# Key-key products of a head moved into its own step of a pipelined delta-rule decoder kernel

## What is computed

```
q = l2norm(causal_conv_silu(x @ Wq)); k, v alike, two of each per token   # 8 heads of 128
beta = 2 * sigmoid(x @ Wb); g = -exp(A_log) * softplus(x @ Wa + dt_bias)
for each token t:
    state = state * exp(g_t)
    for j in range(2):
        u = (v_j - k_j @ state) * beta_j
        state = state + outer(k_j, u)
    o_t = q_t @ state
out = (rmsnorm(o) * norm_w * silu(x @ Wg)) @ Wo
```

## Time and profile before

| | us |
|---|---|
| median of 3 runs | 946.26 |
| the profiled execution | 951.51 |
| its span on the core | 949.5 |
| TensorE busy (matrix products) | 849.2 |
| VectorE busy | 527.4 |
| ScalarE busy | 391.3 |
| POOL busy | 348.5 |

### The profile page before, as it was taken

One profiled execution on the slowest core, in us unless ns is written; L12 is line 12 of the kernel. 1 busy time (PEld: TensorE's weight loads), 2 busy tenths in 40 slices (PEclk: granted clock), 3 DMA queues, 4 the chain that ended last, 5 costly groups with the idle time before them and its releaser, 6 DMA issues.

```text
span 949.5 us, 16704 instructions
## 1 busy us (share of the span) xinstructions
PE 849.2 (89%) x5816; PEld 597.6 (63%) x5817; DVE 527.4 (56%) x1221; ACT 391.3 (41%) x839; POOL 348.5 (37%) x654
## 2 busy tenths in 40 slices
PE   4869999999999999999999876874999999999992
PEld 3344566766766856866667765763666677667762
DVE  3664747878868868878778764465511111111113
ACT  2736746655654654565565323102222222222220
POOL 0158268357555564573682570003330000000005
PEclk9987999999999999999999995797999999999997
DMA  8221230131031021021201301009563001100104
GB/s 206 73 41 27 72 81 8 17 78 17 9 79 23 11 70 23 13 67 24 51 2 23 90 1 28 1 1 374 213 223 134 28 28 33 33 29 26 33 23 127
DMA packets 102595, 57.91 MB, mean 61 GB/s; under 512 B 64192, under 2 KB 98048, under 8 KB 102528
## 3 DMA queue, kind: packets, MB, share of 16 engines
q1 hardware_dynamic: 99488, 51.62, 19.8%
q0 software_dynamic: 1536, 4.20, 1.4%
q10 hardware_dynamic: 1504, 1.20, 0.4%
HBM read 42.45 MB, written 14.55 MB: 60 GB/s over the span
## 4 chain that ended last, share of the span: by engine, by line
PE 76%; DVE 10%; ACT 6%; issue 4%; POOL 2%; DMA 1%; SPq 0%; POOLq 0%; ACTq 0%; DVEq 0%
PE bank L1598 16%; PE bank L581 13%; PE bank L1643 9%; PE bank L715 3%; PE bank L589 3%; DVE y L1053 3%; PE bank L749 3%; PE bank L640 3%; PE bank L700 3%; PE bank L719 2%; PE bank L714 2%; PE bank L595 2%; PE bank L1630 2%; PE bank L674 2%; PE bank L686 2%
## 5 line engine op out<-in xcount | busy, mean ns | idle before, releaser
L1053 DVE SCALAR_TENSOR_TENSOR y<-bank,cwh,y 128x510 f32<-128x510 f32 (+2 forms) x240 | 177.6, 744 | 78.9 <-ACT y L836 75.2
L581 PE MATMUL bank<-xnT,wbuf 128*128 128x512 f32 x320 | 165.2, 642 | 5.3 <-DVE y L1053 4.7
L1598 PE MATMUL bank<-f_wgu,f_xgT 128*128 x368 | 118.8, 466 | 0.0
L1857 DVE TENSOR_TENSOR f_act<-f_sg,bank 128x352 f32<-128x352 f32 x62 | 32.2, 521 | 143.8 <-PE bank L1598 141.4
L1369 POOL TENSOR_TENSOR term<-inv,blk 128x126 f32<-128x126 f32 (+22 forms) x248 | 87.8, 354 | 43.9 <-DMA blk<-a_blocks 25.1
L1932 POOL DMA_INDIRECT f_back<-slots_y,f_slot x16 | 15.4, 963 | 231.4 <-DMA slots_y<-f_yb 224.8
L581 PEld LDWEIGHTS bank<-xnT,wbuf 128*128 128x128 f32 x320 | 57.4, 199 | 66.8 <-issue 53.7
L1372 POOL TENSOR_TENSOR inv<-inv,term 128x126 f32<-128x126 f32 (+22 forms) x248 | 91.6, 369 | 19.4
L1705 ACT ACTIVATE f_sg<-bank 128x352 f32<-128x352 f32 x62 | 28.7, 464 | 161.0 <-PE bank L1598 152.7
L1643 PE MATMUL bank<-f_wdn,f_actT 128*128 (+1 forms) x372 | 91.5, 388 | 0.9 <-ACT f_actT L1718 0.8
L1598 PEld LDWEIGHTS bank<-f_wgu,f_xgT 128*128 128x128 f32 x368 | 66.2, 190 | 36.8 <-issue 7.6
(11 more groups left out here) (208 smaller groups left out, 1585.2 us busy)
## 6 DMA issues: line engine op xcount, KB each, us to landing
f_wgu<-in_exp_gu SPq DMA_DIRECT2D x8, 1408.0 KB, 8.6
f_wdn<-in_exp_dn SPq DMA_DIRECT2D x8, 640.0 KB, 9.7
blk<-a_blocks SPq DMA_DIRECT2D x16, 256.0 KB, 3.9
slots_x<-oT SPq DMA_DIRECT2D x24, 128.0 KB, 1.8
f_xg<-slots_x SPq DMA_DIRECT2D x24, 128.0 KB, 2.0
slots_y<-f_yb SPq DMA_DIRECT2D x23, 128.0 KB, 1.7
a_blocks<-aT SPq DMA_DIRECT2D x64, 32.0 KB, 1.6
inverses<-inv SPq DMA_DIRECT2D x16, 128.0 KB, 3.0
```

Of the source, the lines that this page charges most:

```text
L581: last = mm(bankA[p % 2][:, :], wbuf[A.par][:, kt, wblk, :], xnT[:, kt, (p % 2) * 512:(p % 2 + 1) * 512], start=kt == 0, stop=kt == 1)
L1053: v.scalar_tensor_tensor(out=y[p % 2][:, :, k:], in0=src[:, :, 0:SEQ - k], scalar=cwh[A.par][:, cb, 3 - k:4 - k], in1=y[p % 2][:, :, k:], ...
L1598: last = mm(gu[c][:, 0:FFH], xt[:, k, :], wgu[:, e, k, at:at + FFH], start=k == 0, stop=k == 1)
L1857: v.tensor_tensor(av[:, par, half * FFH:(half + 1) * FFH], sg[:, half, :], gu[2 * half + 1][:, 0:FFH], ALU.mult).then_inc(f_act, 1)
```

## The change

Gram leaves FIRST and is done for head A in slots 9 and 10 of its own step, once its four key projections are through. For this the key norms come two slots sooner (products in pairs behind projections 5 and 7, squares in pairs, sums and beta on VectorE in slot 8), and turn_blocks moves from slot 9 to slot 8, behind them. aT gets two buffers, since head A's products are masked while head B's are still read. p32, t32 and x32 each move a slot ahead, out items 2 and 3 move, kend and gate go one slot ahead. SP's gather is done for A at the step's end, behind scatter(B). POOL's `out_rms` moves into the inversion, ahead of round 12. The lines left out give aT its two buffers, aT0 and aT1, and let the products read `aT[par]`.

```diff
@@ -102,23 +102,24 @@
 FIRST, LAST = "first", "last"
-FILL = {FIRST: {"B": four("gram") + four("qk")},
+FILL = {FIRST: {"B": four("qk")},
         0: {"A": [("dx", 0), ("dx", 1), ("ex", 0), ("ex", 1)]},
...
         5: {"B": [("vtok", 3)]},
-        6: {"B": [("kend", 0)]},
-        7: {"E": [("out", 2)]},
-        8: {"B": [("kend", 1)]},
-        9: {"B": [("gate", 0)]},
-        10: {"B": [("p32", 0), ("p32", 1)], "E": [("out", 3)]},
-        11: {"B": [("t32", 0), ("t32", 1), ("kend", 2)]},
-        LAST: {"B": [("x32", 0), ("x32", 1), ("gate", 1), ("p64", 0), ("p64", 1), ("t64", 0), ("t64", 1)]}}
+        6: {"B": [("kend", 0)], "E": [("out", 2)]},
+        7: {"B": [("kend", 1)]},
+        8: {"B": [("gate", 0)]},
+        9: {"B": [("p32", 0), ("p32", 1)], "A": [("gram", 0), ("gram", 1)]},
+        10: {"B": [("t32", 0), ("t32", 1)], "A": [("gram", 2), ("gram", 3)]},
+        11: {"E": [("out", 3)], "B": [("x32", 0), ("x32", 1), ("kend", 2)]},
+        LAST: {"B": [("p64", 0), ("p64", 1), ("gate", 1), ("t64", 0), ("t64", 1)]}}
 PLACES = [FIRST] + list(range(12)) + [LAST]
...
 B_BANKS = 3
+RMS_AT = 12
@@ -254,6 +255,8 @@
     m8 = sb("m8", [P, 8])
+    aT1 = sb("aT1", [P, BATCH, CH, MU])
+    aT = [aT0, aT1]
     thr = t["thr"]
@@ -436,14 +439,14 @@
-        def gather(B):
+        def gather(A):
             for u in range(2):
-                sp.wait_ge(at_done, 4 * B.h + 2 * u + 2)
+                sp.wait_ge(at_done, 4 * A.h + 2 * u + 2)
                 for q in range(BLOCKS):
                     rows_ = slice(q * NB, (q + 1) * NB)
-                    sp.dma_start(diag[q][:, 8 * u:8 * u + 8, :], aT[rows_, 2 * u:2 * u + 2, :, rows_].rearrange("p b c n -> p (b c) n")).then_inc(a_out, 16)
-            sp.wait_ge(a_out, 32 * BLOCKS * (B.h + 1))
+                    sp.dma_start(diag[q][:, 8 * u:8 * u + 8, :], aT[A.par][rows_, 2 * u:2 * u + 2, :, rows_].rearrange("p b c n -> p (b c) n")).then_inc(a_out, 16)
+            sp.wait_ge(a_out, 32 * BLOCKS * (A.h + 1))
             for k in range(2):
@@ -459,8 +462,6 @@
         def step(A, B, C, E):
-            if B:
-                gather(B)
             if A and A.h < HEADS - 1:
@@ -484,6 +485,8 @@
                 scatter(B)
+            if A:
+                gather(A)
             if s == 1:
@@ -772,12 +775,13 @@
                     mix_turn(slot - 2)
-                if A and 6 <= slot < 10:
-                    norm(A, slot - 6)
                 if s == 0 and slot == 0:
...
                     proj(A, slot)
+                if A and slot in (5, 7):
+                    norm(A, slot - 5)
+                    norm(A, slot - 4)
                 if A and slot == 11:
@@ -875,7 +879,7 @@
                 act.wait_ge(oss_mm, A.h - 1)
-            act.wait_ge(silu_done, 10 * A.h + (4 if i < 4 else 6))
+            act.wait_ge(silu_done, 10 * A.h + (3 if i < 2 else 4 if i < 4 else 6))
             src = kraw[:, i * 512:(i + 1) * 512] if i < 4 else qraw[:, (i - 4) * 512:(i - 3) * 512]
@@ -987,8 +991,9 @@
                     silu(A, slot - 2)
-                if A and 5 <= slot <= 10:
-                    square(A, slot - 5)
+                if A and slot in (4, 6, 8):
+                    square(A, slot - 4)
+                    square(A, slot - 3)
                 if A and slot < 10:
@@ -1114,7 +1119,7 @@
                     dve.wait_ge(dm_done, 2 * B.h + 2)
-                v.tensor_tensor(aT[:, b, :, :].rearrange("p c (t j) -> p (c t) j", j=2), bank.rearrange("p (t j) -> p t j", j=2),
+                v.tensor_tensor(aT[B.par][:, b, :, :].rearrange("p c (t j) -> p (c t) j", j=2), bank.rearrange("p (t j) -> p t j", j=2),
                                 dx[:, b * CH:(b + 1) * CH, :].rearrange("p c (n a) -> p (c n) a", a=1).to_broadcast([P, CH * STEPS, 2]),
@@ -1250,11 +1255,11 @@
                     mix_add(slot - 3)
-                if B and slot == 9:
-                    turn_blocks(B)
-                if A and slot == 10:
+                if A and slot == 8:
                     norm_sum(A, 0)
                     fold_beta(A)
+                if B and slot == 8:
+                    turn_blocks(B)
                 if A and slot == 11:
@@ -1358,11 +1363,13 @@
-        def invert(B):
+        def invert(B, E):
...
             for j in range(NB - 1):
+                if j == RMS_AT and E:
+                    out_rms(E)
                 r, k = j // 2 + 1, NB - 1 - j
@@ -1377,10 +1384,10 @@
                 start(A)
-            if E:
+            if B:
+                invert(B, E)
+            elif E:
                 out_rms(E)
-            if B:
-                invert(B)
             if A:
...
                     pool.wait_ge(scal_done, 4)
```

More of the change, by code:

```diff
@@ L233, in attention @@
     gm = sb("gm", [P, BC // 2, STEPS])
-    aT = sb("aT", [P, BATCH, CH, MU])
+    aT0 = sb("aT0", [P, BATCH, CH, MU])
     TT = [sb(f"TT{i}", [P, BATCH, CH, MU]) for i in range(2)]
@@ L660, in item @@
                 m = n * (BC // 2) + k
-                a_m, t_m = aT[:, m // CH, m % CH, :], TT[par][:, m // CH, m % CH, :]
+                a_m, t_m = aT[par][:, m // CH, m % CH, :], TT[par][:, m // CH, m % CH, :]
                 cols = slice(k * STEPS, (k + 1) * STEPS)
```

## The result

The changed kernel takes 960.16 us (median; 955.31 to 964.43), the kernel before, run beside it on the same chip, 945.99 (943.99 to 947.09). The ratio is 1.0139, with a 95% interval of 1.0091 to 1.0186. The sign of the forecast holds (slower), the size does not: +6.0 us was forecast, +14.2 measured, and 960.2 lies 1.2 us above the range of 942 to 959.

The account below looks back on a forecast made before the run. TensorE was taken to bound the kernel, busy 849.2 of 949.5 us. Terms -4.6 + 1.0 + 9.0 + 0 - 4.5 + 4.5 = +5.4, +6.0 with kend's bank, put on the median 946.3 gave 952.2 us; range 942 to 959.

Parts of the forecast that it names:

- Part 1: Start of step 1: POOL's chain starts sooner, so TensorE's wait for gm shrinks; 4.6 us gained, bounds 2.5 to 5.
- Part 2: Slots 8 and 9: TensorE's p32 waits 1.5 us for X1 in steps 2 to 7, 9.0 us, plus 1.0 in step 1.
- (c): VectorE's slot 8: X1 is in time because TensorE runs later there; 937.7 us, faster; chance 0.10.
- (d): X1's two transposes are slowed by POOL's dx multiplication, 0 to 1.9 us in seven steps; 959 us; chance 0.10.
- Rival (e): Late masks on VectorE keep the inversion from coming forward, step 8 gives nothing; 956.7 us; within the forecast's 0.50.
- Part 3: Step boundary: a wait of 0.7 us replaces the 0.68, the dx wait stays; 0 per step, bounds -0.2 and +0.5.
- Part 4: Reordered queues, such as step 1's similarity tiles behind the gather and the scalars on POOL: no cost, with little cover.
- Part 5: Step 8: the 7.37 us X1 wait goes, a wait for U comes, half clock stays; 4.5 us gained.
- rival (b): Step 8: TensorE's clock is back to full, 9 us less; 943.2 us; chance 0.15.
- Part 6: Middle steps: half-clock stretches behind the new X1 wait, 2.5 x 1.8 = 4.5 us lost, bounds 0 to 10.8.
- Rival (a): Middle steps: waits as forecast, but no half-clock stretch at the new wait; 947.7 us, no change; chance 0.15.

Follow-up runs that it names:

- e3_tiles_first: Changed kernel with SyncE issuing step 1's four similarity-tile DMAs ahead of the gather: 948.96 us, ratio 1.0022 to the kernel before.
- e7_before_late_sel: Kernel before with step 8's second top-k selection on VectorE moved from slot 9 to slot 11: 945.77 us, ratio 0.9963.
- e1_again: The changed kernel run again without any edit: 957.79 us, ratio 1.0116 to the kernel before.
- e2: Changed kernel with X1's transposes ahead of the norm sums and beta in VectorE's slot 8: 952.67 us, ratio 1.0041 to the kernel before.
- e4: Changed kernel with X1 ahead of the norm sums and the similarity tiles' DMAs ahead of the gather: 943.1 us, ratio 0.9931 to the kernel before.
- e11: Changed kernel with tiles ahead of the gather and ScalarE's table load ahead of its dx wait, X1 still behind the norm sums: 942.52 us, ratio 0.9970.
- e8: e4 plus ScalarE's table load ahead of its wait for the dx bank: 928.58 us, ratio 0.9792 to the kernel before.
- e5_all: e4 plus step 8's second top-k selection moved from slot 9 to slot 11: 938.78 us, ratio 0.9852 to the kernel before.

## Why the prediction was wrong, point by point

**Part 1, the start of step 1: right.** Step 0 is 5.0 us shorter (forecast 4.6, bounds 2.5 to 5), and the wait for gm 1.51 us in place of 4.01. POOL's chain starts at 50.17 in place of 57.65; less the 2.5 us by which this profile is early, that is the 52.7 of the forecast.

**Part 2, the wait for X1: right to 0.02 us.** 1.52 in each of steps 2 to 7 and 0.86 in step 1, against 1.5 and 1.0. Rivals (c) and (d) are out: X1 was not in time, and POOL's dx multiplication did not slow its transposes (the pair took 1.43 us from 311.25, with the multiplication beside it from 311.48; before, 1.42). Rival (e) is out too: the inversion came sooner, and step 8's wait for X1 went.

**Part 3, the boundary: 0 was a little too high.** A step at full clock and without the X1 wait is 0.5 us shorter than before (66.40 and 66.87), which is outside the bounds of -0.2 and +0.5. The wait for mq is 0.46 us in place of the 0.68 for the masked bank. The rest was not traced to its cause. og kept its length beside the inversion, a median of 1.285 us and at most 1.431, so the 2.1 us that could have come did not. What was drawn out is POOL's instruction beside it, 1.39 us where one of its shape takes 0.33, and likewise in all six steps (1.2 to 1.4 in place of 0.3 to 0.4):

```profile
196.57 1.28 DVE L1201 SCALAR_TENSOR_TENSOR og<-oT,normw,gate 128x1024 f32<-128x1024 f32 x1 [1.28 <-ACT osq L891]
```
```profile
196.66 1.39 POOL L1376 TENSOR_TENSOR term<-inv,blk 128x81 f32<-128x81 f32 x1
```

This agrees with the Trainium skill, "SBUF — State Buffer", "Who interferes with whom", by which the earlier issue goes on and the other waits: here og was the earlier one, and POOL, for which no one on TensorE's path waits there, paid. qn, which stood beside POOL's qE, fell from 1.525 to 0.171 us in the median, but that of step 0 still stands beside qE and took 2.644.

**Part 4, the queues: this step failed.** It said of the tiles behind the gather: "nothing, with little cover". In the kernel before the tiles were issued from 105.40 us on, and POOL did not wait for them. The other times in Part 4 were nearly right. The tiles were issued from 118.03, 3.0 us before the q-k products' start at 120.99 (forecast: some 2), and POOL needs 5.2 us from the memset to the end of gm. What the sum left out is the transfer's landing:

```profile
118.03 2.68 SPq L428 DMA_DIRECT2D similarities<-TT  x4
```
```profile
123.75 1.80 POOL L1351 MEMSET TT<- 128x2048 f32 x1 [14.81 <-DMA similarities<-TT]
...
127.89 1.04 POOL L1291 TENSOR_TENSOR gm<-g_sb,masks 128x512 f32<-128x512 f32 x1
```

From the first issue until the memset may start 5.7 us pass. So gm is ready at 128.9, 7.9 us behind 120.99 and not 3.4, and dx 0 waits 4.30. That wait and the half clock behind it are what e3_tiles_first took back: 8.8 us, as much as the whole error of the forecast (14.2 - 6.0 = 8.2) within the noise. Of the other terms, Part 3 missed by some -3 us over six steps and Part 5 by +2.2, which nearly cancel.

**Part 5, step 8: half the gain, -2.3 for -4.5.** The X1 wait of 7.37 us went and U's came, 2.96 us, as forecast. What the sum lacked stands in the first two of these rows, and U's wait in the third:

```profile
587.79 1.16 PE L703 MATMUL bank<-R,TT 128*128 128x128 f32 x8 [2.52 <-ACT oT L963]
590.58 1.92 PE L673 MATMUL bank<-TT,P 32*32 32x32 f32 x64 [1.63 <-ACT P L943]
595.45 0.69 PE L717 MATMUL bank<-qE,S 128*128 128x64 f32 x2 [2.96 <-DVE R L1166]
```

The wait for oT is 0.6 us longer than before, and the one for P is new: with p32 early there is nothing between it and t32 in a step without projections. In all, the step's waits fell from 17.9 to 14.4 us, and TensorE's busy time for the same 405 instructions grew by 1.1 us, which leaves the 2.3. The clock of the step was 0.74 (before 0.73) and was at half behind the selection as before, so rival (b) is out.

**Part 6, the clock: right in kind; half of the size in the sum, and mostly from other waits.** The forecast was 4.5 us, for 2.5 stretches more. With 67.94 us for a step of the changed kernel at full clock and 66.87 for one of the kernel before, steps 3 to 6 lost 4.5 and 3.4 us to half clock; step 7 lost another 4.5 us (72.16 against 66.58 + 1.07), and before nothing. That is 5.6 more. Step 2 lost 5.5 (70.78 against e3_tiles_first's 65.30) where the kernel before lost 1.7 (66.62 against 64.90 at full clock, the profile of e7_before_late_sel): 3.8 more. In all 9.4.

By what stands ahead of it, the time at half clock in steps 2 to 7 of this profile is 10.1 us behind the wait for gm, 6.8 behind two of the X1 waits, 3.4 behind a dx wait, and 13.7 behind a wait of 0.61 us for mq; before, it was 10.2 behind three dx waits. So the two X1 stretches (some 3.4 us lost) are near what the forecast took for them, and over all profiles 10 of 24 such waits had one, against its 3 in 6. The terms that it lacked are the stretch behind gm, which comes of Part 4, and the one behind mq, which the profile of e1_again does not have and which thus belongs to this execution.

What the forecast did not see either is that these prices don't add: taking the X1 waits away gave 5 to 9 us (e1 to e2 and e3 to e4: 5.1 and 5.9 by the medians, 7.1 and 8.6 by the ratios) while the dx waits stood, and 14 to 17 with the dx waits gone (e11 to e8), though one wait of 4.1 us for X1 was left in step 1. The two ranges are some 5 us uncertain each, so this is likely, not shown.

Rival (a), no half clock behind the new wait, is out, and so is its reason: waits of 0.54 and 0.61 us were followed by it too.

## What stays open

Why the half clock follows the dx waits in all six steps of e5_all and in none of e3_tiles_first is not settled. The wait is 1.11 us in both, and the work behind it is the same. The 2.4 us by which the part behind step 8 was longer in the profile after were not followed either.

## What to carry to other kernels

When a queued transfer is moved behind another, cost its landing and not only its issue, and follow the landing to the engine whose buffer it frees: here four transfers issued from 3 us ahead of the step boundary on, in place of 19, became a TensorE wait of 4.3 and some 4 us more at half clock. When two instructions change places on an engine that is not the bottleneck, ask which of them the bottleneck wants first: two swapped lines were 1.5 us a step. Judge a reordering with its own new waits and the old short ones removed: it went from 1.2% slower to 0.5 to 0.9% faster (ratios 0.9792, with X1 and the tiles put first, and 0.9845, both with the table load moved; medians 928.58 and 937.04 us, five runs each on one chip, so it is hardly clear of the noise).

## What the runs showed of the hardware

TensorE's clock went to its lower level (1.2 of 2.4 GHz) behind waits of 1.1 and 1.5 us in 34 of 74 cases, and at waits of 3.0 us in 6 of 6. In the four middle steps of three kernels whose longest wait there is 0.7 us, it never did, though elsewhere it fell behind waits of 0.54 and 0.61. A stretch of 3.4 us costs 1.6 to 1.8 us. Executions of one kernel on one core differ by up to 18 us (e4_both: 932.86 to 950.69), and the granted clock that each run reports orders them nearly as the time does. Taking 1.11 us waits for a table load from the start of the steps was worth 14.7 us to the kernel before (1.55%, uncertain by 4.6), more than its 8.0 us of waits.
